# A graph layer with a recurrence on one core: edges in tiles of 128, the first stage reordered, the norm stage by node, one prefix pass behind the recurrence

## The reference, cut to what matters

```python
xn = _layernorm(x, axis=-1)
# graph block
neigh = jax.ops.segment_sum(xn[src], dst, num_segments=n)
h = (1.0 + eps) * xn + neigh
h = relu(h @ W1 + b1) @ W2 + b2
h = (h - mean(h, 0)) * rsqrt(var(h, 0) + 1e-5) * gamma + beta
# attention block on xn: q, k, v by head; k and v normalized by head
kv = einsum('bhnd,bhne->bhde', k, v) / n
ret = einsum('bhnd,bhde->bhne', q, kv) + xn
m = gelu(ret @ w1 + b1, approximate=False) @ w2 + b2 + xn
x = x + h + m
# recurrence on the normalized sum
s = lstm(_layernorm(x))                      # 6250 steps, state of 256
g = argmax(s @ W_lin.T + b_lin)              # 0 or 1 for each node
w = g * s
inc = cumsum(w, axis=1)
out = x + 2.0 * s + (inc - w) * fw_att + (inc[:, -1:] - inc) * bw_att
```

## Time and profile before

| | us |
|---|---|
| median of 3 runs | 16860.86 |
| lowest and highest | 16857.71, 16862.74 |
| the profiled execution | 16838.88 |
| its span | 16837.2 |

### The profile page before, as it was taken

How to read it: one execution, slowest core, us unless ns; L and a number is a source line. 1 busy time by engine, 2 the same in 40 slices (tenths; PEclk the granted TensorE clock), 3 DMA queues, 4 the chain that set the end, 5 groups by cost and what they waited for, 6 DMA issues and landing times. The chain is left out here.

```text
span 16837.2 us, 921205 instructions
## 1 busy us (share of the span) xinstructions
PE 12623.9 (75%) x375188; PEld 11631.8 (69%) x375188; DVE 10192.6 (61%) x84227; ACT 5185.6 (31%) x32373; POOL 2589.9 (15%) x1609
## 2 busy tenths in 40 slices
PE   3333344468888888888888888888888888888887
PEld 2222233348888888888888888888888888888886
DVE  4433211266666666666666666666666666666667
ACT  1000000133333333333333333333333333333333
POOL 4888888600000000000000000000000000000000
PEclk6666666675555555555555555555555555555555
DMA  5444444410000000000000000000000000000000
GB/s 140 71 72 72 67 68 68 80 62 1 1 1 1 1 1 1 1 1 1 1 1 1 1 1 1 1 1 1 1 1 1 1 1 1 1 1 1 1 1 16
DMA packets 923352, 317.17 MB, mean 19 GB/s; under 512 B 755540, under 2 KB 875112, under 8 KB 923315
## 3 DMA queue, kind: packets, MB, share of 16 engines
q0 software_dynamic: 435200, 207.54, 8.2%
q1 hardware_dynamic: 464589, 98.59, 3.2%
q10 hardware_dynamic: 23526, 10.59, 0.3%
HBM read 150.06 MB, written 150.93 MB: 18 GB/s over the span
## 5 line engine op out<-in xcount | busy, mean ns | idle before, releaser
L1261 PE MATMUL bank<-hrest,whh 128*128 128x1 bf16 (+1 forms) x300000 | 9077.1, 166 | 1920.3 <-DVE hrest L1385 1920.3
L1261 PEld LDWEIGHTS bank<-hrest,whh 128*128 128x128 bf16 x300000 | 8548.9, 104 | 2481.0 <-DVE hrest L1385 2480.6
L1329 ACT ACTIVATE gates<-bank 128x4 f32<-128x4 f32 x12500 | 2183.5, 175 | 8141.6 <-DVE bank L1366 7254.0
L1366 DVE TENSOR_REDUCE bank<-bank 128x4 f32<-128x12 f32 x12500 | 2210.0, 177 | 3186.0 <-PE bank L1261 2300.4
L1261 PE MATMUL bank<-xsteps,wih 128*128 128x15 bf16 (+1 forms) x60048 | 2714.9, 174 | 0.0
L1374 DVE CUSTOM_DVE_ANT_1 uv<-gates 128x4 f32<-128x4 f32 x12500 | 2041.3, 163 | 450.1
L1261 PEld LDWEIGHTS bank<-xsteps,wih 128*128 128x128 bf16 x60048 | 2277.1, 104 | 0.0
L1337 ACT ACTIVATE bank<-gates 128x1 f32<-128x1 f32 x12500 | 2176.9, 174 | 124.8
L1390 DVE TENSOR_TENSOR hrest<-hrest 128x1 f32<-128x1 f32 x12500 | 1987.4, 159 | 216.2
L1395 DVE TENSOR_TENSOR hrest<-hrest 128x1 f32<-128x1 f32 x12500 | 1961.2, 157 | 217.1
L1261 PE MATMUL bank<-ones,gbias 128*128 128x5 bf16 x10008 | 1678.6, 168 | 18.6 <-DMA xsteps<-x_d 18.6
(11 more groups left out here) (167 smaller groups left out, 3726.3 us busy)
## 6 DMA issues: line engine op xcount, KB each, us to landing
acc_d<-zero SPq DMA_DIRECT2D x40, 637.5 KB, 14.5
ht<-acc_d SPq DMA_DIRECT2D x100, 224.0 KB
xsteps<-x_d SPq DMA_DIRECT2D x1252, 7.5 KB, 1.7
U<-hrest SPq DMA_DIRECT2D x1250, 5.0 KB, 1.7
rows<-xn_d,staged_i POOLq DMA_INDIRECT x800, 4.0
acc_d<-sums,target POOLq DMA_INDIRECT x800, 6.1
x_d<-x SPq DMA_DIRECT2D x25, 375.0 KB, 2.3
xk<-U SPq DMA_DIRECT2D x50, 125.0 KB, 5.0
```

Source lines behind the costliest of these rows:

```text
L1261: return nc.tensor.matmul(to, w, v, start=start, stop=True, skip_group_check=True)
L1329: nc.scalar.activation(gates[:, k, 0:2 * NG_[k]:2], zi[k], ACT.Tanh).then_inc(ifg_act[k], 1)
L1366: nc.vector.tensor_reduce(zi[k], gi[k][b][:, s], axis=AX.X, op=ALU.add).then_inc(ifg_summed[k], 1)
```

## The change

Groups of edges are now 4 x 128: 195 full groups and one last group of 160 edges as two tiles of 80. The loops of the second edge block are cut so that the last chunk of nodes carries no group. In the first stage, ten of the 24 constants are loaded by ScalarE at its very beginning, ahead of the square root; the issues of `xn_d` move to SP and are woven with 30 of the 40 zero transfers. PE and VectorE wait in the first edge block for the ten loads alone, and for the other fourteen at the second block's start. The seven weight loads of the graph block move from SP to ScalarE. In the norm stage the variance is a product with `csq` as the stationary operand, so it comes out as 125 x 2, the inverse root is made on that shape, and two transposes spread it over 128 partitions; the parts are made by VectorE alone as float32 numbers whose upper half is the bf16 part, and `x2_d` and `xsteps` hold float32. In the last stage `pre` is gone: the forward pass subtracts `fw * w`, and the prefix enters once, on ScalarE, with the factor `fw - bw`.

```diff
-NG = E // (R * GT)
+RE = 128
+NG = E // (RE * GT)
+LAST = (80, 2)
-MIX_LOADS = 24
+MIX_LOADS, LATE_LOADS = 10, 14
...
-                for a in range(NA):
-                    flat = acc_d[a].rearrange("n d -> (n d)").rearrange("(p w) -> p w", p=128)
-                    for j in range(ZS):
-                        sp.dma_start(flat[:, j * ZW:(j + 1) * ZW], zero[:]).then_inc(zero_out[a], 16)
...
+                for piece in range(ZS):
+                    zeros(piece)
+                piece = ZS
+                for t in range(NT):
+                    sp.wait_ge(xn_ready, t + 1)
+                    for lo, hi in SPLIT:
+                        sp.dma_start(xn_d[t * R + lo:t * R + hi, :], xn[lo:hi, t % XB, :]).then_inc(xn_out[t % XB], 16)
+                    if t % 5 in (0, 2, 4):
+                        zeros(piece)
+                        piece += 1
...
+                assert len(ld) == MIX_LOADS
+                for to, v in ld:
+                    act.dma_start(to, v).then_inc(mixw_in, 16)
+
                 act.wait_ge(var_ready, 1)
                 nc.scalar.activation(root[:], var[:], ACT.Sqrt).then_inc(root_ready, 1)
...
-                        act.wait_ge(xn_ready, t + 1)
-                        for lo, hi in SPLIT:
-                            act.dma_start(xn_d[bass.ds(t * R + lo, hi - lo), :], xn[lo:hi, b, :])\
-                               .then_inc(xn_out[b], 16)
...
                 def variance(c):
                     pe.wait_ge(csq_ready, c + 1)
                     if due(c):
-                        pe.wait_ge(rs_ready, c)
-                    for k in range(KD):
-                        last = nc.tensor.matmul(bank[2][:, 0:C], avg[:], csq[:, k, :], start=k == 0, stop=k == KD - 1)
+                        pe.wait_ge(nvar_ready, c)
+                    for j in range(2):
+                        for k in range(KD):
+                            last = nc.tensor.matmul(bank[2][0:R, j:j + 1], csq[:, k, j * R:(j + 1) * R], avg[:, 0:1],
+                                                    start=k == 0, stop=k == KD - 1)
                     last.then_inc(var_made, 1)
 
+                def root_rows(c, b):
+                    pe.wait_ge(nrs_ready, c + 1)
...
+                    for j in range(2):
+                        last = nc.tensor.transpose(bank[3 + b][:, j * R:(j + 1) * R],
+                                                   nrs[:, b, j:j + 1].broadcast_to([R, 128]), ident[0:R, 0:R])
...
-            xs_ = sb("xsteps", [128, 2, KD, B, PARTS], BF16, st)
+            xs_ = sb("xsteps", [128, 2, PARTS, KD, B], F32, st)
+            xs_hi = xs_[:].bitcast(BF16).rearrange("p b c k (t e) -> p b c k t e", e=2)[:, :, :, :, :, 1]
...
-                                yield to[:, :, 0:PARTS - p], wih[:, p, k, cols], xs_[:, b, k, :, 0:PARTS - p], False
+                                yield to[:, :, 0:PARTS - p], wih[:, p, k, cols], xs_hi[:, b, 0:PARTS - p, k, :].rearrange("p c t -> p t c"), False
...
-                    nc.vector.tensor_tensor(XT[:, :, at], XT[:, :, at], states(c), ALU.add).then_inc(sum_ready, 1)
+                    for k in range(KD):
+                        stt(out=XT[:, k, at], in0=wgt[:, k, :], scalar=minus_fw[:, k:k + 1], in1=XT[:, k, at],
+                            op0=ALU.mult, op1=ALU.add).then_inc(base_ready, 1)
...
-                    nc.vector.tensor_tensor(pre[:], inc[:, :, at], wgt[:], ALU.subtract).then_inc(pre_ready, 1)
...
-                    for k in range(KD):
-                        dve.wait_ge(suf_ready, 2 * c + k + 1)
-                        stt(out=fin[:, b, k, :], in0=suf[:, b, k, :], scalar=bw[:, k:k + 1], in1=XT[:, k, at],
-                            op0=ALU.mult, op1=ALU.add).then_inc(fin_ready, 1)
+                    nc.vector.tensor_tensor(XT[:, :, at], XT[:, :, at], states(c), ALU.add).then_inc(sum_ready, 1)
+                    dve.wait_ge(sum_ready, c + 1)
+                    dve.wait_ge(suf_ready, 2 * c + 2)
+                    nc.vector.tensor_tensor(fin[:, b], suf[:, b], XT[:, :, at], ALU.add).then_inc(fin_ready, 1)
```

More of the change, by code:

```diff
@@ L231, in _ @@
                 first_apart(act, NT // XB, body)
-                for b in range(XB):
-                    act.wait_ge(xn_out[b], 32 * (NT // XB))
             @block.vector
@@ L337, in stage_group, with gather_group @@
                 sp.sem_inc(sp_turn)
[L338 to L342 removed]
+                for m, (v, rest) in enumerate(((src_g, src_l), (dst_g, dst_l))):
+                    part = v[bass.ds(2 * h + g, 1)].rearrange("q p t -> p (q t)") if of == FULL else rest
+                    sp.dma_start(staged_i[0:P, g, m, 0:T], part).then_inc(staged[g], 16)
+            def gather_group(pool, h, g, first=False, of=FULL):
+                P, T = of
                 pool.wait_ge(staged[g], 32 * (h + 1))
@@ L671, in gps_layer_kernel, with chunk_groups, last_apart @@
             block = open_block()
+            HL = NG // 2
+            assert HL == H2 + 2 * (NC - 2) + 1
+            def chunk_groups(i):
+                h = 2 * i + H2
+                if isinstance(i, int) and i == NC - 1:
+                    return ()
+                return ((h, 0, FULL), (h, 1, FULL), (h + 1, 0, FULL),
+                        (h + 1, 1, LAST if isinstance(i, int) and i == NC - 2 else FULL))
+            def last_apart(engine, body):
+                body(0)
+                with engine.Fori(1, NC - 2, 1) as i:
+                    body(i)
+                body(NC - 2)
+                body(NC - 1)
             def view(b):
@@ L688, in _ @@
                 gather_group(pool, H2, 0)
[L689 removed]
+                with pool.Fori(H2, HL, 1) as h:
                     gather_group(pool, h, 1)
@@ L1059, in _ @@
                 variance(0)
+                mean(2, 0)
+                variance(1)
                 skewed(pe, step)
@@ new lines, in step @@
+                    if more:
+                        variance(c + 1, 1 - b)
+                    if within(c + 3):
+                        residual(c + 3)
+                    if more:
+                        inverse(c + 1, 1 - b)
+                    scaled(c, n, b)
+                    if more:
+                        inverse_square(c + 1, 1 - b)
+                    if within(c + 2):
+                        center(c + 2, b)
+                    if more:
+                        correction(c + 1, 1 - b)
@@ L1164, in _ @@
+                    first_rest(c, b)
+                    if more:
+                        corrected(c + 1, 1 - b)
+                    second_rest(c, b)
                 residual(0)
@@ L1166, in _ @@
                 center(0, 0)
+                residual(2)
+                center(1, 1)
+                variance(0, 0)
+                inverse(0, 0)
+                inverse_square(0, 0)
+                correction(0, 0)
+                corrected(0, 0)
                 skewed(dve, step)
-                first_rest(NC - 1, (NC - 1) % 2)
-                third_part(NC - 1, (NC - 1) % 2)
             @block.sync
@@ L1581, in forward @@
                         weigh(c + 1)
-                    dve.wait_ge(pre_ready, c + 1)
-                    dve.wait_ge(sum_ready, c + 1)
-                    for k in range(KD):
-                        stt(out=XT[:, k, at], in0=pre[:, k, :], scalar=fw[:, k:k + 1], in1=XT[:, k, at],
-                            op0=ALU.mult, op1=ALU.add).then_inc(fwd_ready, 1)
                 choose(0)
```

412 lines of the change are left out of this document (219 added, 193 removed).

## The result

| | us |
|---|---|
| before, median of 4 runs | 16860.62 (16857.71 to 16862.74) |
| with the change, median of 4 runs | 16120.88 (16115.91 to 16126.16) |
| ratio, 95% interval | 0.9561 (0.9545 to 0.9578) |
| profiled executions | 16838.88, then 16118.48 |

The kernel is 740 us faster by the medians. The forecast was 240 us, and its range went down to 16570: the sign was right and the size was not, by a factor of three. The profiled executions lie 22 us (before) and 2 us (with the change) under the medians, so the traces share out 720 us. One of six executions of one kernel further down (whole rows, issued by SP) took 16931.94 us, at a granted clock of 1.00 where the other five have 0.54, and its median leaves that one out.

A forecast was written before the change was run, and what follows sets the result against it. The recurrence is 77% of the span but barely touched; POOL's issue paces the edge blocks. Terms -59 - 67 - 3 - 100 + 0 - 11 = -240 us give 16621 us for the median, range 16570 to 16690.

The forecast's parts named there:

- The groups: Edge blocks: 18 gathers and 18 scatters fewer, each costing the same with 128 rows as with 125; -67 us.
- cost by row: Edge blocks, a rival: indirect transfers cost by row, so 58 us of the gain gone, 16679 us; chance 0.12.
- The first stage: Start to first scatter: no wait for the last constants, but a later root at 60 us; -59 us, between -42 and -73.
- rival 3: First stage: ScalarE's loads starve behind x and ten zeros, root at 77 us, 17 us more, 16638 us; chance 0.20.
- Graph block: Graph block: seven loads move from SP to ScalarE, no longer ahead of the accumulators; -3 us, 0 to -4.6.
- Norm stage: Norm stage: a step falls from 9.33 to about 5.1 us, a loop over three engines; -100 us, between -74 and -124.
- Recurrence: Recurrence: strided reads of `xsteps` by the input products are covered by PE's 0.30 us wait for the state; 0 us.
- Rival 1: Recurrence: the strided operand slows the input products and the kernel gets slower, at worst +1715 us, 18336 us; chance 0.05.
- Last stage: Last stage: forward pass loses `pre` and a sum, a chunk takes 4.1 us against 4.5; -11 us, 0 to -27.

The follow-up runs named there:

- whole rows, issued by SP: Changed kernel with kv_g and kv_b loaded once, not per head, and all constant loads as whole rows; SP issues both pieces of xn_d: 16072.05 us.
- rows125: Changed kernel with edge tiles of 125 rows in place of 128, as many transfers, 2340 edges left out: 16633.4 us.
- kernel with short loads: Changed kernel with kv_g and kv_b loaded once, not once for each of eight heads: 16069.71 us, 0.9543 of before.

## Why the prediction was right or wrong

**The groups (-67, measured -569).** The step that failed is "544 = 16 x 34; 125 rows don't divide over 16 engines, 128 do, so the descriptors are already made for 128", with which the term put the change in a transfer's price at nothing. The price fell instead, from 1.235 to 0.999 us for a gather and from 2.001 to 1.595 for a scatter, and that is 502 us. The packet count was the right row to look at and the inference from it was wrong. That 544 divides by 16 says nothing of how the rows were cut: 176, 656 and 2576 divide by 16 too. The sign was its size: 250 rows (125 read, 125 added) need 160 packets with data and 32 of 4 bytes, and 352 more were there, which carry none. The comparison that I made had two ends, equal cost or cost by row, and neither lets the price of a transfer fall. The count of transfers was right: 69 us of it came as forecast. rows125 shows the rest, 508 us by its trace.

**The first stage (-59, measured -21).** The root came at 79.6 us, as in rival 3 (77), which had the term at -42; its reason holds only in part. The short runs were not shut out beside x and the zeros: 5987 of the 10096 were through by 52 us. From 0 to 20 us ScalarE's queue moved 3276 of them beside 3773 runs of SP, nearly one for one, and from 20 to 32 us 1284 beside 2388. With the rule of the Trainium skill, "DMA: Bandwidth & Descriptors", section "Queues, rings and completion order", that each DMA engine goes round robin between its queue rows, the trace agrees in the first of these stretches. What came late were the runs left at 52 us, some 107 in a microsecond. The root was 19.6 us later than in the sum, and from it to the first scatter it took 110.7 us where the sum had 92.5. Of these 18 us the wait of 16.47 us behind the fifth tile is the main part: an issue that ends is not a transfer that has landed, and the packets left in the queues held `xn_d`. My sum also had 75 us from the root to the stage's end; in the kernel with short loads it is 84 us from the root to the first gather, and the DMA engines are 0.90 to 0.94 busy at 315 to 330 GB/s there, not at the 391 of the earlier trace rows, which is for the zeros with few other transfers.

**Graph block (-3, measured 0).** `ht` is issued 4.6 us earlier in the block now, but beside ScalarE's weights, and its sum starts 11.2 us into the block where it started 10.9 us into it before. Within the range.

**Norm stage (-100, measured -105).** The loop over three engines is as worked out. Timeline:

```profile
2986.61 0.16 DVE L1184 TENSOR_SCALAR nvar<-bank 125x2 f32<-125x2 f32 x1 [1.21 <-PE bank L1099]
...
2989.79 1.84 PE L1099 MATMUL bank<-avg,csq 128*125 128x1 f32 x8
...
2991.67 0.16 DVE L1184 TENSOR_SCALAR nvar<-bank 125x2 f32<-125x2 f32 x1 [1.21 <-PE bank L1099]
```

This step is 5.06 us and the next 4.92, in turn through the middle of the stage, 5.0 in the mean (5.1 forecast, 9.33 before; the first and last few steps are 4.8 and less). The variance's eight passes take 1.84 us (1.6 taken, between 0.2 and 2.7), and VectorE waits 1.21 us for them. That the step came out right is partly luck: the variance was 0.24 us longer than taken, the handovers between the engines shorter by about as much. The passes run at the low clock (0.50 in the window of the stage).

**Recurrence (0, measured 0.0).** Two programs that were profiled twice had recurrences 12 and 13 us apart, and over all traces its length moves by 26 us, so the 0.0 is exact by chance; a cost of the strided operand over some 4 ns a step would stand out and does not. PE waits 1914.7 us in all for the new state, 1920.3 before, and the 60048 input products with the strided operand take 174 ns each in the records, as before. Rival 1 is out, and no row shows the penalty by 16-byte lines that the Trainium skill, "SBUF — State Buffer", section "Door 1: The DMA port swizzle (why `[64,N]` ≈ `[32,N]`)", led me to weigh.

**Last stage (-11, measured -25).** The term that was too small is the forward chunk: the sum had it at 4.1 us, a mean over both clocks. It measured 3.46: with the instructions gone PE's idle time shrank and the clock stayed up. The far end of the term's range, 27 us, was this case.

Without the price of the rows the change would have brought 720 - 502 = 218 us by the trace, near the 240 of the sum, and in part by luck: the groups' term was too small by 502 us, the first stage's too large by 38 and the graph block's by 3, the last stage's and the norm stage's too small by 14 and 5.

## What to carry to other kernels

Give an indirect transfer a number of rows whose largest divisor up to 16 is 16 or 15. A tile of 125 or 127 rows, taken for a round count of tiles, cost more here than the ragged rest that 128 leaves, because GpSimd's issue was the pace. When a count in the profile doesn't fit a simple picture (here 544 packets for 250 rows), work out what it would be under each theory before it is used as evidence for one. Loads of a thousand runs of 128 bytes don't belong ahead of anything that others wait for: make the runs long, or load once and repeat by the access pattern.

## What was not expected of the hardware

- An indirect transfer of 127 rows takes GpSimd 2.57 us (gather) and 4.75 us (scatter), one of 128 rows 1.00 and 1.60 us; 16 rows more or less at the same divisor are worth 0.02 and 0.10 us.
- In all seven kernels with 112 to 128 rows the software queue gets as many packets as 16 equally long shares would make. Shares without rows are filled with packets of 4 to 16 bytes: none at 128 rows, 352 for a pair at 125, 2385 at 127.
- Loads of 1000 runs of 128 bytes hold the issuing engine 7.5 to 9.8 us each with the DMA engines busy to 0.06 to 0.09, and with such packets still in the queues another queue's transfer was waited for 16 us longer.
- The recurrence, one program and the same 6250 steps, took 12888.6 us in one execution and 12900.4 in another.
- A 0.67 us instruction on VectorE cost 1.0 us a chunk, 0.3 of it in chunks where TensorE's granted clock was low.
